# The gate rows of two MoE stages, from 128 partitions to 40

## The reference

```python
# sixth (L2_ffn): top 2 of 8 experts
probs = softmax(x @ router_w.T)
weights, indices = top_k(probs, 2)
weights = weights / (weights.sum(-1) + 1e-6)
h = silu(gate) * up            # gate, up = split(x @ w13[e]), 256 wide
y = sum over e of weight[e] * (h @ w2[e])
# eighth (L3_ffn): experts until the sum of probabilities reaches 0.8
probs = softmax(x @ Wr + br)
gate = probs * keep
y = sum over e of gate[e] * (relu(x @ W1[e] + b1[e]) @ W2[e] + b2[e])   # 512 wide
```

## Time and profile before

| | |
|---|---|
| median of 3 runs | 2750.63 us (2746.95 to 2752.39) |
| the profiled execution | 2752.39 us |
| its span, first to last instruction | 2750.6 us |
| PE busy | 2411.4 us, 88% |
| PEld, DVE, ACT, POOL busy | 65%, 68%, 54%, 35% |
| stage 6, stage 8 | about 1431 to 1738 us, about 2327 to 2733 us |

### The profile page before, as it was taken

One profiled execution on the slowest core, in us unless ns is written; L12 is line 12 of the kernel. 1 busy time (PEld: TensorE's weight loads), 2 busy tenths in 40 slices (PEclk: granted clock), 3 DMA queues, 4 the chain that ended last, 5 costly groups with the idle time before them and its releaser, 6 DMA issues. The chain is left out here.

```text
span 2750.6 us, 35026 instructions
## 1 busy us (share of the span) xinstructions
PE 2411.4 (88%) x12122; PEld 1782.2 (65%) x12122; DVE 1873.0 (68%) x3501; ACT 1472.2 (54%) x3113; POOL 970.0 (35%) x769
## 2 busy tenths in 40 slices
PE   5778677699799999999989999688888887899998
PEld 2556466588688888888877888333333333677776
DVE  6745555677566566666657666388888887777776
ACT  4331122389444444444445666555656554788887
POOL 1000000021222222222204555488888886222222
PEclk8668798899899999999989999899999998999999
DMA  4000000000000000000010000122222221000001
GB/s 177 0 1 0 1 1 0 1 1 1 16 1 1 1 1 1 1 1 1 1 62 1 1 1 9 36 84 82 81 80 82 82 82 46 1 1 1 1 1 31
DMA packets 31169, 66.85 MB, mean 24 GB/s; under 512 B 3200, under 2 KB 7312, under 8 KB 30480
## 3 DMA queue, kind: packets, MB, share of 16 engines
q1 hardware_dynamic: 30960, 64.59, 7.6%
q0 software_dynamic: 32, 0.02, 0.0%
HBM read 61.98 MB, written 2.62 MB: 23 GB/s over the span
## 5 line engine op out<-in xcount | busy, mean ns | idle before, releaser
L192 PE MATMUL ps<-TMPr 128*128 128x512 f32 (+5 forms) x3936 | 982.1, 403 | 64.8 <-DVE TMPr L208 34.1
L192 PEld LDWEIGHTS ps<-TMPr 128*128 128x128 f32 (+3 forms) x3936 | 738.8, 192 | 319.3 <-issue 110.3
L212 POOL TENSOR_TENSOR TMP<-TMP 128x512 f32<-128x512 f32 (+2 forms) x480 | 611.8, 1299 | 683.0 <-ACT TMP L203 466.1
L192 PE MATMUL ps<-TMP 128*128 128x65 f32 (+5 forms) x4352 | 546.6, 293 | 1.2 <-DVE TMP L207 0.5
L192 PEld LDWEIGHTS ps<-TMP 128*128 128x128 f32 (+3 forms) x4352 | 488.7, 193 | 69.6 <-issue 28.0
L203 ACT ACTIVATE TMP<-ps,W 128x256 f32<-128x256 f32 (+2 forms) x528 | 283.5, 584 | 343.5 <-DVE TMP L208 193.3
L192 PE MATMUL ps<-TMP,W 128*128 128x512 f32 (+5 forms) x720 | 377.4, 648 | 101.6 <-POOL TMP L212 39.9
L208 DVE TENSOR_TENSOR TMP<-ps,TMP 128x512 f32<-128x512 f32 (+1 forms) x434 | 251.7, 604 | 119.2 <-PE ps L192 59.3
L192 PEld LDWEIGHTS ps<-TMP,W 128*128 128x128 f32 (+3 forms) x720 | 128.7, 196 | 271.2 <-issue 143.4
L203 ACT ACTIVATE TMPr<-ps,W 128x512 fp32r<-128x512 f32 x352 | 242.8, 690 | 89.7 <-PE ps L192 70.3
L212 POOL TENSOR_TENSOR XT<-XT,XK 128x512 f32<-128x512 f32 x128 | 176.0, 1375 | 299.9 <-DVE XK L211 286.4
(11 more groups left out here) (186 smaller groups left out, 2752.5 us busy)
## 6 DMA issues: line engine op xcount, KB each, us to landing
TMP<-rows SPq DMA_DIRECT2D x168, 256.0 KB, 3.6
W<-wp SPq DMA_DIRECT2D x1, 4124.0 KB, 13.3
W<-wp SPq DMA_DIRECT2D x1, 3072.0 KB, 25.3
W<-wp SPq DMA_DIRECT2D x1, 2136.5 KB, 18.6
XT<-xT SPq DMA_DIRECT2D x4, 512.0 KB, 6.1
out<-XK SPq DMA_DIRECT2D x8, 256.0 KB, 2.3
W<-wp SPq DMA_DIRECT2D x1, 1993.0 KB, 14.1
W<-wp SPq DMA_DIRECT2D x1, 903.0 KB, 9.8
```

The costliest lines, as they stand in the source:

```text
L192: return nc.tensor.matmul(out, lhsT, rhs, start=start, stop=stop, **k)
L212: gtt = lambda o, a, b, op: nc.gpsimd.tensor_tensor(o, a, b, op)
```

## The change

The rows of the gates are kept on 40 partitions instead of 128, end to end: the constant `sel16r`, `s8` and `WT` have 40 partitions, the transposes read 40 columns and write 40 partitions of bank 0, ACT copies these 40, and the gate matmul contracts over 40 rows. `WKR` has 320 columns instead of 408. No wait, no step and no order is changed.

```diff
-    [("ss2", 64, 32), ("sel16r", 128, 8), ("ones", 128, 128), ("one64", 64, 1), ("hm", 128, 16),
+    [("ss2", 64, 32), ("sel16r", 40, 8), ("ones", 128, 128), ("one64", 64, 1), ("hm", 128, 16),
...
-        WT, WK = ar(T, dt=FR), ar(64)
+        WT, WK = ar(T, 40, FR), ar(64)
...
-        s8 = ar(8, dt=FR)
+        s8 = ar(8, 40, FR)
...
-        WKR = [rt(408, dt=FR) for _ in range(2)]
+        WKR = [rt(320, dt=FR) for _ in range(2)]
...
-                wkr = g3(WKR[b % 2][:, 0:320], 8)
-                high, low = wkr[:, :, 0:8], wkr[:, :, 32:40]
+                high, low = g3(WKR[b % 2], 8)[:, :, 0:8], g3(WKR[b % 2], 8)[:, :, 32:40]
...
-                tt(low, wk, g3(WKF[b % 2][:, 0:320], 8)[:, :, 0:8], ALU.subtract).then_inc(*sig("low"))
+                tt(low, wk, g3(WKF[b % 2], 8)[:, :, 0:8], ALU.subtract).then_inc(*sig("low"))
...
-                        r = turn(tile(PS[0], j), WKF[i // 2 % 2][:, c * 40:c * 40 + 128], w("ident"))
+                        r = turn(tile(PS[0][0:40, :], j), WKF[i // 2 % 2][:, c * 40:c * 40 + 40], w("ident"))
...
-                    mm(PS[0], s8[:, x:x + 1].to_broadcast([128, 128]), ch(WT, i)).then_inc(*mg_pe(a))
+                    mm(PS[0], s8[:, x:x + 1].to_broadcast([40, 128]), ch(WT, i)[0:40, :]).then_inc(*mg_pe(a))
...
-                    acopy(ch(WT, a[1]), PS[0]).then_inc(*mw_act(a))
+                    acopy(ch(WT, a[1])[0:40, :], PS[0][0:40, :]).then_inc(*mw_act(a))
...
-    c["sel16r"] = np.concatenate([np.eye(8), np.zeros((24, 8)), np.eye(8), np.zeros((88, 8))], 0)
+    c["sel16r"] = np.concatenate([np.eye(8), np.zeros((24, 8)), np.eye(8)], 0)
```

## The result

The changed kernel takes 2795.84 us (median of 4 runs, 2779.53 to 2799.69); the kernel before, on the same chip, 2749.52 us (2746.95 to 2752.39). The ratio is 1.0166, with a 95% interval of 1.0147 to 1.0184: 1.7% slower, where 2797 was forecast. The profiled execution of the changed kernel took 2796.76 us, its span is 2795.0 us.

The account below looks back on a forecast made before the run. PE was taken to set the pace in stages 6 and 8, one matmul per 0.232 us. Gates 49.9, less 3.1 for first experts, plus 0 for transposes gave +46.8 us: 2797 us, range 2776 to 2809 (about 0.85).

Parts of the forecast that it names:

- What bounds the kernel: Stages 6 and 8: PE sets the pace, one matmul every 0.232 us; shortening ACT, DVE or POOL work moves nothing.
- 40 rows are treated like 64: Gate matmuls in stages 6 and 8: 40 rows switch the array's division like 64, costing 0.39 us each.
- The rival of full-size gates: Gate matmuls: 40 rows act as full-size, no drain, sum 0, 2748 to 2753 us; chance 0.12.
- The price of 0.39 us: Each of 128 gates: going in and coming out loses 0.39 us, read from 64-row matmuls in stage 7; 49.9 us.
- The first expert: First expert of stages 6 and 8: PE waits for DVE's routing, so half its gates' cost vanishes, 3.1 us in all.
- The stall in stage 8 takes up nothing: Stage 8's 1.34 us stall per expert, while DVE makes the next weights, absorbs no gate loss; later gates delay DVE too.
- The transposes, copies and memsets: Row transposes, ACT's PS-to-WT copies and POOL's memsets: counted at 0; transposes bounded by 2.6 us gained, 6.2 us lost.
- The sum: Whole kernel: 49.9 - 3.1 + 0 = +46.8 us, 2797 us on the median, +1.7%.
- The signs in the profile: Stages 6 and 8: gates' mean near 500 ns, PEld idle over 0.3 us before each, stages about 24 us longer each.
- some 410 matmuls: Stage 6: a 100 us window of the changed kernel's profile would hold some 410 matmuls instead of 433.

Follow-up runs that it names:

- e6: The kernel before with each 128-row gate matmul issued twice in a row; 2779.45 us, ratio 1.0099 to the kernel before.
- e4: The changed kernel with each 40-row gate matmul issued twice in a row; 2818.13 us, ratio 1.0224 to the kernel before.
- e3: The changed kernel with the gate matmul back at 128 rows and WT zeroed once per stage; 2757.70 us, ratio 1.0009 to the kernel before.
- e8: The kernel before with DVE making the next expert's weights in four pieces after chunks 1 to 4, first expert excepted; 2746.45 us, ratio 0.9974.
- e10: The changed kernel with DVE making the next expert's weights in four spread pieces, first expert excepted; 2784.23 us, ratio 1.0115 to the kernel before.

## Why the prediction was right

- **What bounds the kernel.** Right. PE's matmuls set both stages; e6 adds one plain matmul per chunk and the time follows.
- **40 rows are treated like 64.** Right, and now shown: 40 and 64 rows give one period, 72 rows that of before. The rival of full-size gates, and with it the sentence of the Trainium skill on a single matmul of 32 rows (TensorE: Matmul & The Clock Gate, closing table), is not what happens with 40 rows between full-size matmuls; a second gate behind a gate adds 0.234 us, about what a plain one costs, as e4 shows. No gate of these runs has 32 rows. The Trainium skill, TensorEngine Tiling (Array Packing), Tiling Modes, is borne out by e4: the drain is paid on a change of mode and not on the use of a tile.
- **The price of 0.39 us.** Right: 0.38 over nine matmuls in one place, 0.385 from the period of stage 6. That it was seen beside slower fp32 matmuls made no difference.
- **The first expert.** The prediction let half of its gates vanish, 3.1 us. Nearly all did: 3.1 us in each of the two stages, so this term was half of what it should have been. PE's idle time from 1445 to 1490 fell from 5.8 to 3.9 us, which is 1.9 of them. DVE's routing sets that stretch; this is read from the waits and was not tested by itself.
- **The stall in stage 8 takes up nothing.** Wrong, by some 2.5 us. The prediction held that the gate ahead of the burst delays the burst too. The profile after shows otherwise:

```profile
2480.96 0.75 DVE L211 SCALAR_TENSOR_TENSOR TMPr<-ps,SM,XK 128x512 fp32r<-128x512 f32 x1 [0.64 <-ACT XK L203]
2481.63 0.74 DVE L211 SCALAR_TENSOR_TENSOR XK<-ps,W,XK 128x512 f32<-128x512 f32 x1
2482.29 1.85 DVE L207 CAST TMPr<-W 128x512 fp32r<-128x512 f32 x2
...
2486.70 0.96 PE L192 MATMUL ps<-TMPr 128*128 128x512 f32 x3 [0.92 <-DVE TMPr L211]
```

  DVE starts the burst behind two of its own instructions, the first of which waits for ACT and not for PE. The gate that stands at that place in PE's order (2480.92, its copy by ACT at 2481.61) is the next chunk's: DVE's product with a gate starts at 2481.63, when that copy has only begun. So DVE doesn't wait for it, PE comes 0.39 us later to the point where it must wait for DVE, and the stall is 0.92 us instead of 1.34. Six experts take up 2.5 us. e8 and e10, which have no stall, differ by 49.49 - 46.45 = 3.04 us per expert against 2.77 with it.
- **The transposes, copies and memsets.** Right: nothing (e3).
- **The sum.** 49.9 less 3.1 were predicted for the span, and 49.9 less 8.3 are found in the two stages (41.6), where the prediction had 46.8. That the median came within 1.2 us of the forecast is partly luck: some 3 us of the longer span lie in a stage that nothing here touches, so the hit is better than the working.
- **The signs in the profile.** The gates' mean (495 ns), PEld's idle time before them and the 0.50 us of the matmul behind each came as said. The "some 410 matmuls" in 100 us of stage 6 was worked out wrongly: by the prediction's own price 19 matmuls take 19 x 0.232 + 0.39 = 4.80 us, which gives 396, and 399 are there. The stages grew by 21.7 and 20.0 us and not by 24 each, and a chunk of stage 8 went from 5.99 to 6.33 us, stalls included, where the prediction had 5.8 and 6.2 without them.

## What to carry to other kernels

Where PE sets the pace, look at the rows of every small matmul that stands between full ones. Here one of 40 or 64 rows cost two changes of division, 0.39 us on top of the 0.23 of a plain matmul, and padding with zeros to 72 rows was free; no number of rows between 64 and 72 was tried. If small ones are needed, put them next to one another, so that the change is paid once. And when a matmul is taken off PE, look for the longest piece of work on the engine that feeds it: that piece can become the next wait. Here taking the gates off alone gave 0.4%, splitting DVE's piece alone 0.3%, and both together 1.1%.

## What the runs showed of the hardware that was not expected

A matmul of 64 rows costs the same as one of 40, and one of 72 within 0.1% of the period the same as one of 128: periods of 38.35 and 38.35 us, and of 35.31 against 35.27. A second matmul with the same 128-row weights right behind the first costs 0.22 us in the period of stage 6, where the plain distance is 0.232. A transpose with 40 stationary columns has loads of 104 ns for 150 and no drain (before, then after):

```profile
L199 PEld LDWEIGHTS ps<-W,XKr 128*128 128x128 f32 x32 | 3.9, 150 | 10.4 <-DVE XKr L208 6.1 <-issue 3.4 <-ACT XK L206 0.5
...
L199 PEld LDWEIGHTS ps<-W,XKr 128*40 128x40 f32 x32 | 3.0, 104 | 8.8 <-DVE XKr L208 6.0 <-issue 1.8 <-ACT XK L206 0.2
```
